# Attention and routed experts on one core: the shared expert's first products, a gate and a router in another order

## The reference, cut to what matters

```
x = layernorm(x + attention(x))
scores = sigmoid(x @ gate_w.T)                 # 32 experts in 8 groups of 4
idx, w = top 6 of the experts in the top 4 groups;  w = w / sum(w) * 2.5
y = sum over the 6 of  w * (silu(x @ w11[e].T) * (x @ w33[e].T)) @ w22[e].T
shared = silu(x @ sw1.T) * (x @ sw3.T) @ sw2.T
x = layernorm(x + y + shared)
```

## Time and profile before

| | |
|---|---|
| median of 3 runs | 649.18 us |
| lowest and highest | 644.78 and 650.74 us |
| the profiled execution's own time | 648.27 us |
| its span in the profile | 646.1 us |
| TensorE busy | 501.8 us (78%) |
| VectorE busy | 354.3 us (55%) |
| ScalarE busy | 331.1 us (51%) |
| GpSimd busy | 222.2 us (34%) |

### The profile page before, as it was taken

The page is one execution under the profiler, slowest core; times in us unless marked ns, Lnnn a source line. Parts: engine busy times, 40 slices in busy tenths (PEclk is TensorE's granted clock), DMA queues, the critical chain, the costliest instruction groups (busy, mean ns, idle before and its releaser), DMA issues.

```text
span 646.1 us, 11869 instructions
## 1 busy us (share of the span) xinstructions
PE 501.8 (78%) x2806; PEld 381.0 (59%) x2807; DVE 354.3 (55%) x1744; ACT 331.1 (51%) x1093; POOL 222.2 (34%) x244
## 2 busy tenths in 40 slices
PE   5287777677686748575489899899999999987584
PEld 3165565455564626363155588787787877865562
DVE  3144759284664929295145355555555555543496
ACT  1188978375674838370020265565565655545033
POOL 0000000606143250607606054655555655545000
PEclk9679989879686968688969999999999999999697
DMA  4877598837382730308884345444444545420993
GB/s 128 193 193 223 128 260 231 237 96 196 92 200 87 177 108 32 123 7 305 322 335 179 84 135 145 139 146 140 148 144 140 156 148 156 146 73 18 374 416 120
DMA packets 67991, 107.87 MB, mean 167 GB/s; under 512 B 9189, under 2 KB 55018, under 8 KB 66416
## 3 DMA queue, kind: packets, MB, share of 16 engines
q1 hardware_dynamic: 54016, 75.15, 40.8%
q0 software_dynamic: 10752, 26.13, 11.6%
q10 hardware_dynamic: 3184, 6.13, 2.5%
HBM read 64.03 MB, written 43.33 MB: 166 GB/s over the span
## 4 chain that ended last, share of the span: by engine, by line
PE 49%; DMA 12%; ACT 11%; DVE 10%; issue 9%; another core or an unknown queue 6%; SPq 2%; POOL 1%; ACTq 0%; POOLq 0%; DVEq 0%
PE bank L695 16%; PE bank L711 9%; ACT probs L808 6%; DMA expert_w<-expert_out 5%; PE bank L636 4%; PE bank L687 4%; ACT pT L819 2%; PE bank L539 2%; DMA k_scratch<-k_lo 2%; DMA k_pack<-k_scratch 2%; DVE s_neg L986 2%; PE bank L476 2%; PE bank L703 2%; PE bank L645 2%
## 5 line engine op out<-in xcount | busy, mean ns | idle before, releaser
L1346 POOL DMA_INDIRECT routed<-rows,position x96 | 93.6, 975 | 259.1 <-DVE position L1137 231.5
L1356 POOL DMA_INDIRECT expert_out<-ey_all,out_row x128 | 126.0, 984 | 114.8 <-issue 80.6
L808 ACT ACTIVATE probs<-s_neg,m_neg 128x128 f32<-128x128 f32 (+1 forms) x256 | 114.0, 453 | 78.2 <-DVE m_neg L986 55.3
L695 PE MATMUL bank<-expert_w,xgT 128*128 x512 | 132.5, 381 | 5.0 <-issue 4.6
L986 DVE CUSTOM_DVE_ANT_0 s_neg<-bank,bias_sb 128x128 f32<-128x128 f32 (+1 forms) x256 | 78.2, 352 | 95.6 <-PE bank L508 47.9
L695 PEld LDWEIGHTS bank<-expert_w,xgT 128*128 128x128 f32 x512 | 87.3, 190 | 23.1 <-issue 7.6
L911 ACT ACTIVATE ey_all<-bank,pick 128x256 f32<-128x256 f32 x128 | 60.6, 473 | 57.8 <-PE bank L711 50.2
L711 PE MATMUL bank<-expert_w,eaT 128*128 x256 | 79.8, 393 | 5.7 <-DVE eaT L1283 4.0
L1262 DVE SCALAR_TENSOR_TENSOR pick_of<-xg,slot_e 128x12 f32<-128x12 f32 x128 | 29.8, 233 | 94.6 <-ACT eg L905 85.6
L508 PE MATMUL bank<-k_pack,q_pack 128*128 128x256 f32 (+1 forms) x128 | 61.1, 486 | 15.0 <-DMA k_pack<-k_scratch 11.5
L522 PE MATMUL bank<-cst,probs 128*128 128x128 f32 x256 | 48.4, 316 | 21.6 <-ACT probs L808 16.8
(11 more groups left out here) (155 smaller groups left out, 736.4 us busy)
## 6 DMA issues: line engine op xcount, KB each, us to landing
xg<-routed SPq DMA_DIRECT2D x128, 137.5 KB
expert_w<-expert_out SPq DMA_DIRECT2D x16, 768.0 KB
expert_w<-expert_weights SPq DMA_DIRECT2D x9, 1024.0 KB, 11.4
q_pack<-q_scratch SPq DMA_DIRECT2D x32, 256.0 KB
routed<-empty SPq DMA_DIRECT2D x8, 550.0 KB, 12.1
k_pack<-k_scratch SPq DMA_DIRECT2D x16, 256.0 KB
expert_w<-expert_weights ACTq DMA_DIRECT2D x3, 1024.0 KB
xt<-xT SPq DMA_DIRECT2D x9, 256.0 KB, 6.9
```

The lines of the kernel that those rows point to most:

```text
L695: last = pe.matmul(S_BANK[k % 2][:, 0:2 * INTER], xgT[k % 4][:, c, :], w13_sb[c][:, bass.ds(e, 1), :].rearrange("p a n -> p (a n)"), start ...
L808: act.activation(probs[g % 2][qb][:, 2 * pair + r, :], s_neg[u][:, r, 0:n], ACT.Exp, bias=m_neg[:, u, r:r + 1], scale=-1.0, accum_out=row_ ...
L1346: pool.indirect_dma_start(routed, bass.IndirectOffsetOnAxis(ap=position[b % ROW_BUFS][:, t, j:j + 1], axis=0), rows[b % ROW_BUFS][:, t, :] ...
L1356: pool.indirect_dma_start(expert_out, bass.IndirectOffsetOnAxis(ap=out_row[:, k:k + 1], axis=0), ey[k], None, bounds_check=TOKENS * TOPK - ...
```

## The change

The same instructions run, in another order on three engines, between loop and slots alone. On TensorE the first `shared_up` goes ahead of batch 6's `ranks`; batch 7's `gate` and `shared_down(0)` go ahead of `shared_up(1, 0)`; and `ranks` of batch 7 goes ahead of `shared_up(1, 1)`. On ScalarE the first `shared_silu` goes ahead of batch 7's logarithm and exponential, and `shared_silu(1, 0)` behind `gate_exps`. On VectorE `shared_act(0, 0)` goes between the two halves of the layer norm, the adds of block 0 go in pairs between the router's parts, and part 3 goes ahead of the `shared_act` of block 1.

```diff
             project_out(last_b, 1)
+            shared_up(0, 0)
             ranks(last_b - 1, 0)
-            shared_up(0, 0)
             shared_up(0, 1)
             turn_x1(last_b, 1)
-            shared_up(1, 0)
             gate(last_b, 1)
             shared_down(0)
+            shared_up(1, 0)
+            ranks(last_b, 1)
             shared_up(1, 1)
-            ranks(last_b, 1)
             shared_up(2, 0)
...
             gate_exps(last_b - 1)
+            shared_silu(0, 0)
             ln_first_root(last_b)
-            shared_silu(0, 0)
             shared_silu(0, 1)
             copy_x1t(last_b, 1, last_b // 2)
-            shared_silu(1, 0)
             gate_exps(last_b)
             load_weights(act, W_GROUPS - 1)
+            shared_silu(1, 0)
             shared_silu(1, 1)
...
             ln_stats(b, 1, b // 2)
+            shared_act(0, 0)
             ln_apply(b, 1, b // 2)
-            shared_act(0, 0)
             shared_act(0, 1)
             router(b, 1, 0)
+            shared_add(0, range(0, 2))
             router(b, 1, 1)
-            shared_add(0)
+            shared_add(0, range(2, 4))
             router(b, 1, 2)
+            router(b, 1, 3)
             shared_act(1, 0)
             shared_act(1, 1)
-            router(b, 1, 3)
```

More of the change, by code:

```diff
@@ L1182, in shared_act, with shared_add @@
                 dve.tensor_tensor(sh_a[m][:], T_BANK[m][:], sh_g[m][:], ALU.mult).then_inc(sh_act, 1)
[L1184 to L1187, removed]
+            def shared_add(tb, tiles=range(4)):
+                if 0 in tiles:
+                    for i in range(2):
+                        dve.wait_ge(x1_kept[i], 32 * (tb + 1))
+                for t in tiles:
                     tile = x_sum[:, 4 * tb + t, :]
```

## The result

| | before | after |
|---|---|---|
| median of 20 runs each | 650.85 us | 652.57 us |
| lowest and highest | 644.06 and 653.62 us | 646.75 and 657.47 us |
| the profiled execution's own time | 648.27 us | 652.32 us |
| its span | 646.1 us | 650.1 us |

The ratio of after to before is 1.0043, with a 95% interval from 1.0022 to 1.0064. The change costs 0.4%: 1.7 us between the medians, 2.8 us by the ratio, which leaves out the slowest execution of after (657.47 us) because it ran in a slower state. The forecast was 647.1 us, a gain of 1.2. The time lies in the range and within 1% of before, but on the other side.

What follows compares the result with a forecast made beforehand. The bound was TensorE's chain to the last add, its completions held while scatters run. Earlier copy - 4.2, shared_up(1, 0) behind the gate + 3.6, a wait regained - 0.6: - 1.2 us from 648.27 gives 647.1 us, range 638 to 655.

Steps and rivals of the forecast that it cites:

- The bound: Between loop and slots: TensorE's chain to the last add at 366.62 ends last; ahead of the gate, its held completions.
- `shared_up(0, 0)` ends ahead of batch 6's scatter and should pass: Ahead of the gate: the moved product, 297.1 to 300.7, has its completion seen without a hold.
- are not late: Batch 6's ranks on TensorE, at 301.11, are not delayed by the 3.6 us product moved ahead of them.
- The table loads: ScalarE ahead of the gate: three more loads of 1.28 us, one on the layer norm's chain, the other two hidden.
- let go at 319.6: Transposes' completion ahead of the gate: second in line, not third, so the copy starts 4.2 us before 323.8.
- let go early: Rival, chance 0.18: transposes' completion let go at 311.0 to 315, gate 9 to 12.8 us earlier, total 642 to 634 us.
- + 3.0 us in all: TensorE behind the gate: shared_up(1, 0) adds 3.6 us, the wait of 0.58 us comes back, clock as before.
- slower than before: Rival, chance 0.10: shared_down(1) and its adds fall deeper into batch 7's scatter, one hold 3.1 to 10.5 us; 654.4 to 661.8 us.

Runs made afterwards that it cites:

- e11: Kernel before with only ScalarE's and VectorE's part of the change's head, TensorE's first shared_up staying behind batch 6's ranks: 647.29 us, ratio 1.0014 to before.
- e5: Kernel before with only the change's head: shared_up, shared_silu and shared_act (0, 0) moved, order behind the gate as before: 644.55 us, ratio 0.9984 to before.
- e2: Kernel after, with the scatters of batches 6 and 7 waiting until all adds are done: 680.29 us, ratio 1.046 to before.
- e1: Kernel before, with the scatters of batches 6 and 7 waiting until all adds are done: 680.27 us, ratio 1.0434 to before.
- e6: Kernel after, with shared_up, shared_silu and shared_act (0, 0) put back, so only the change's tail remains: 656.26 us, ratio 1.0147 to before.
- e10: Kernel after, with batch 7's scatter waiting for the ones product that feeds the counts: 646.23 us, ratio 0.9995 to before.
- e7: Kernel before, with GpSimd waiting in every scatter after each 4 of 12 DMAs until those issued have landed: 616.15 us, ratio 0.9529 to before.
- e8: Kernel after, with GpSimd waiting in every scatter after each 4 of 12 DMAs until those issued have landed: 617.6 us, ratio 0.956 to before.
- e9: Kernel before, with GpSimd waiting after each 4 of 12 scatter DMAs until they landed, for batches 0 to 5 alone: 606.45 us, ratio 0.9372 to before.
- e4: Kernel after, with batch 6's scatter waiting for batch 7's copy_x1t: 660.35 us, ratio 1.0134 to before.

## Why the prediction was wrong, point by point

**The bound.** Right: TensorE's chain up to the last add decided the time, and held completions were what could move it.

**"`shared_up(0, 0)` ends ahead of batch 6's scatter and should pass"; the ranks "are not late".** This step failed. I had looked at the scatters of batches 6 and 7, and not at batch 5's, which was still being issued until 304.96 (and until 305.01 in before, where I could have seen it). The product came in its last part, was held until 307.08, and the ranks behind it with it. e11 against e5 shows it: with TensorE's order as before `picked` waits 0.38 us, with the new one 5.87. Why one product is held where the small ranks alone, as deep in the same scatter, are not, is open.

**The table loads.** Right in size: from logarithm to exponential it took 312.00 - 310.49 = 1.51 us, of which the load is 1.28. The Trainium skill, "ScalarE: Activation LUTs", section on what a table load costs, adds a drain of 1380 ns to each switch; no row here shows one. It did not matter beside the 5 us by which the norm came late for the reason above.

**The completion of the transposes, "let go at 319.6".** Failed, to the good: it was let go at once. I had extrapolated a pattern of places in a line (4.2 us, then 10.5). The rows point to two other things: how far into a scatter a completion falls, and whether there was a gap ahead of that scatter. The late ranks made a gap between the scatters of batches 5 and 6 (304.96 to 308.83); what had been held was let go, and the transposes, which ended 6.4 us into the next scatter, passed. Before, they ended only 4.1 us into it, but with a gap of 1 us, and were held. The copy's time is that of the rival "let go early" (311 to 315 us, measured 315.25), but neither its reason, fewer completions in the line, nor its total, 634 to 642 us, came true.

**Behind the gate, "+ 3.0 us in all".** This step failed, and it is the one that turned the sign: it was + 12.0. The sum had no term for completions held behind the gate; that stood in a rival alone. The order by itself costs nothing: from the gate 42.6 us in e2 against 43.0 in e1. In e6, whose gate is as late as before, `shared_down(1)` starts 0.6 us later behind the gate, not 3.0. The rest was given back by the clock, which I had expected to stay at half as long as before. It came back sooner: e6's clock by stretch (columns as rows 7) shows it, where before it was 0.50 until 334:

```profile
328.00:331.00 3.00, 3.00 (x10) 2.44 (x9) 1.78 (x11) 1.28 (x1) 0.00 (x0) 0.65 0.90 371
331.00:335.00 4.00, 4.00 (x13) 2.10 (x12) 3.73 (x18) 0.00 (x0) 0.00 (x0) 1.00 1.02 430
```

Why it came back sooner is not shown. That the wait of 0.58 us at 330.54 was gone does not explain it, for e11 has the same wait, and its clock is back all the same (1.99 us for the products that took 3.78 before):

```profile
327.49 1.99 PE L645 MATMUL bank<-sw_sb,sh_a 128*128 128x256 f32 x8 [0.58 <-DVE x_sum L1190]
```

The 54.2 us of after exceed e2's 42.6 by 11.6. Measured from the gate, `shared_up(1, 0)` starts 3.8 us later than in e2 (326.99 - 315.90 = 11.1 against 323.26 - 316.00 = 7.3; the held second add); batch 7's ranks 2.1 more (half clock); the product behind `shared_down(1)` 4.1 more (the held third and fourth adds); and `shared_down(2)` 1.5 more (half clock again). That is 11.5. The first two, 5.9 us, follow from batch 6's scatter, which the late ranks had pushed to 308.83 to 323.83 while the early gate brought `shared_down(0)` to 317.63, deep into it. The last two, 5.6 us, follow from batch 7's scatter.

**The rival "slower than before"** named half of the mechanism: `shared_down(1)` deeper in batch 7's scatter. I gave it 0.10. e6 shows it with a late gate: 7.6 us, inside its 3.1 to 10.5 for one hold (the 3.1 is 356.61 - 353.4 = 3.2). The depth came out right there by luck of two errors: the scatter starts 4.0 us sooner behind the gate, not 1.6, and `shared_down(1)` 0.6 us later, not 3. In after the scatter doesn't come sooner at all: it starts 18.6 us behind the gate, against 16.5 before, as the held add of block 0 stands ahead of the router and a `shared_up` at half clock ahead of the ranks; `shared_down(1)` comes 27.2 us behind the gate, against 20.5. e10 shows this half the other way round. The other half, the hold of block 0's add in batch 6's scatter, stood in no rival.

What I had not seen either is that a hold and the early gate would come together: - 8.56 and + 12.04 us make the 3.5. I had treated as rivals what one cause, the start of batch 6's scatter, brings about at once. That the time lies in the range is luck: the misses against the forecast, - 4.4 us at the gate and + 9.0 behind it, had opposite signs.

## What to carry to other kernels

A wait put down to nothing, far behind the end of the producer, is to be laid beside the DMA issues of every engine, from the first one still running, before a product is moved. A product that fills an idle hole can make a short product behind it late: here it filled 4.0 us and the ranks' result came 5.7 us later (307.14 against 301.44 for `picked`). In the whole that cost nothing that was measured (e5), since it also moved the next scatter. And where a queue's traffic holds completions, look to the traffic first: GpSimd waiting for its own DMAs gave up to 6.3%, while no reordering here moved the time by more than 1.5%.

## What the runs showed of the hardware

I had not expected TensorE's completions to be held for up to 13 us while GpSimd issues indirect DMAs. A scatter of 12 DMAs takes 15.1 us to issue. Completions that fell in its first 8 us were mostly prompt; later ones were mostly held and let go around its end, up to 2.9 us behind it. Between two scatters, held completions are let go in a gap of 3.9 us (after); with one of 1 us the next scatter holds them from its start on (in before, a product that ended at 306.26 was seen at 310.48). Once GpSimd waits for its DMAs after every four, the longest wait of this kind in the loop is 4.0 us (e7, e8) and 5.8 us (e9).

They seem to leave in order: the ranks in after, ended at 301.3, left with the product ahead of them, at 307.1, and likewise in e2, e4, e5 and e10. The Trainium skill, "TensorE: Matmul & The Clock Gate", part 3 on packing small matmuls, says that matmuls start and end strictly in order; the rows agree, and suggest that the order holds for what the other engines see as well.

Two waits of this kind were hardly touched: `l_rows` on VectorE, 4.0 us in before and in e7, and `v_sb` on ScalarE, 6.1 us in before and 5.8 us in two waits in e7. What limits the completions, the number of outstanding DMAs or of their descriptors, or something that these share, is not settled; in the loop, parts of 6 leave more holds than parts of 4. The exact place in a scatter from which a hold begins isn't settled either: wherever the ranks come first, they passed 11 us into batch 5's scatter.
